# Two-layer graph attention: layer 1's scores from fp16 parts, its pipeline deepened by one row, one subtraction moved to GpSimd

## The reference

```python
h = jnp.maximum(_layernorm(x, axis=-1), 0.0)
q, k, v = split_heads(h @ Wq), split_heads(h @ Wk), split_heads(h @ Wv)
sim = jnp.einsum('bhid,bhjd->bhij', q, k) * scale
sim = jnp.where(adjacency_mask[:, None, :, :], sim, neg)
attn = jax.nn.softmax(sim, axis=-1)
out = jnp.einsum('bhij,bhjd->bhid', attn, v)     # heads side by side again
x = x + out @ Wo + bo
```

## Time and profile before

| | |
|---|---|
| median of 3 runs | 2652.82 us (2652.71 to 2655.8) |
| the profiled execution | 2656.29 us, span 2654.5 us |
| PE busy | 2587.7 us, 97% of the span |
| DVE busy | 1990.9 us, 75% |
| ACT busy | 1754.5 us, 66% |
| POOL busy | 1399.6 us, 53% |
| share of 16 DMA engines | 69.0% |

### The profile page before, as it was taken

One profiled execution on the slowest core, in us unless ns is written; L12 is line 12 of the kernel. 1 busy time (PEld: TensorE's weight loads), 2 busy tenths in 40 slices (PEclk: granted clock), 3 DMA queues, 4 the chain that ended last, 5 costly groups with the idle time before them and its releaser, 6 DMA issues. The chain is left out here.

```text
span 2654.5 us, 62516 instructions
## 1 busy us (share of the span) xinstructions
PE 2587.7 (97%) x20882; PEld 1393.6 (52%) x20886; DVE 1990.9 (75%) x6361; ACT 1754.5 (66%) x5020; POOL 1399.6 (53%) x2790
## 2 busy tenths in 40 slices
PE   6999999999999999999999999997999999999998
PEld 3455555555555555555555555554555555555554
DVE  6477778777877777777777777786777777777766
ACT  3566666666666666666666666675777777777774
POOL 4255545545554555555555555544565656555552
PEclk9999999999999999999999999998999999999999
DMA  5367766776667666766776677678786777778774
GB/s 141 61 136 158 144 135 133 149 155 130 145 141 140 145 128 144 149 142 133 141 147 141 131 140 146 148 141 195 158 175 160 169 163 170 164 160 170 158 149 102
DMA packets 945489, 387.43 MB, mean 146 GB/s; under 512 B 857617, under 2 KB 859153, under 8 KB 945169
## 3 DMA queue, kind: packets, MB, share of 16 engines
q1 hardware_dynamic: 945168, 383.44, 69.0%
HBM read 114.86 MB, written 67.11 MB: 69 GB/s over the span
## 5 line engine op out<-in xcount | busy, mean ns | idle before, releaser
L552 ACT ACTIVATE probs<-probs,negmax 128x128 f32<-128x128 f32 x1024 | 398.2, 390 | 455.6 <-DVE negmax L124 455.6
L465 POOL TENSOR_TENSOR o_sb<-o_sb,xres 128x512 f32<-128x512 f32 x127 | 161.5, 1272 | 496.5 <-DVE o_sb L739 493.1
L166 PE MATMUL l_ps_pj<-hT,room 128*128 128x512 f16 x1488 | 346.7, 383 | 2.3 <-ACT room L1343 2.3
L166 PE MATMUL ps_pj<-wm_hi,hT 128*128 128x512 f16 x1024 | 326.4, 380 | 12.6 <-DVE wm_lo L761 6.8
L166 PE MATMUL ps_pj<-wv_hi,hT 128*128 128x512 f16 x1024 | 326.4, 380 | 0.0
L166 PE MATMUL ps_pj<-hT,wk_hi 128*128 128x512 f16 x1024 | 305.9, 380 | 0.0
L166 PE MATMUL ps_pj<-hT,wq_hi 128*128 128x512 f16 x1024 | 304.5, 379 | 0.0
L1357 ACT ACTIVATE l_probs<-l_probs,l_negmax 128x128 f32<-128x128 f32 x512 | 199.2, 390 | 139.0 <-DVE l_negmax L124 138.8
L1292 POOL TENSOR_TENSOR l_h<-l_h 128x512 f16<-128x512 f32 x120 | 139.6, 1164 | 282.3 <-DVE l_out_sb L1440 245.0
L124 DVE CUSTOM_DVE_ANT_0 probs<-ps_sc,mask 128x128 f32<-128x128 f32 x1024 | 235.4, 285 | 47.4 <-PE ps_sc L981 46.7
L721 DVE SCALAR_TENSOR_TENSOR c<-cprobs,c 128x512 f16<-128x512 f32 x256 | 185.2, 723 | 79.6 <-ACT c L559 79.2
(11 more groups left out here) (172 smaller groups left out, 6198.8 us busy)
## 6 DMA issues: line engine op xcount, KB each, us to landing
xg<-in_x SPq DMA_DIRECT2D x128, 256.0 KB, 3.4
xres<-in_x SPq DMA_DIRECT2D x128, 256.0 KB, 3.1
x_scratch<-o_sb SPq DMA_DIRECT2D x128, 256.0 KB, 2.4
out<-l_out_sb SPq DMA_DIRECT2D x128, 256.0 KB, 3.3
l_ring<-x_scratch SPq DMA_DIRECT2D x124, 256.0 KB, 3.2
mask_u<-in_adj SPq DMA_DIRECT2D x64, 64.0 KB, 2.8
cpT<-c SPq DMA_TRANSPOSE x256, 3.2
xg<-x_scratch SPq DMA_DIRECT2D x12, 256.0 KB, 3.2
```

What stands on the lines that cost most here:

```text
L166: last = pe.matmul(out, a(kt), b(kt), start=(n == 0), stop=(n == 3 * kts - 1))
L465: nc.gpsimd.tensor_tensor(o_sb[:, j % 2], o_sb[:, j % 2], xres[:, j % 2], ALU.add).then_inc(res_done, 1)
L552: last = nc.scalar.activation(probs[:, i], probs[:, i], ACT.Exp, bias=negmax[:, u % 2, i:i + 1], scale=-1.0, accum_out=zsum[:, u % 4, hh:h ...
```

## The change

The scores of layer 1 are made of three fp16 products per pair of heads in place of one f32 product. For that the projections of q and k are no longer scaled and copied in f32: ScalarE writes their high part (`qk_high`), VectorE the low part (`qk_low`), and the scale is applied in `mask_scores`. The mask's value for excluded pairs is scaled to match. Projections run five rows ahead (`LEAD`), h one row further ahead, `weigh_values` three rows behind (`LAG`). The probabilities have four places instead of one (`nprobs`) and two (`p16`), v has three groups of places, the ring of rows 22 places. The factor 2^14 on the probabilities is applied through the reciprocal, for which `normalise` has one more small multiply. `p_low` is an instruction of GpSimd, first in its pass. The `factors` stand in the passes with n % 4 == 0.

```diff
 # numbers of places and passes
-RING = 20
+RING = 22
+LEAD = 5
+LAG = 3
 # mask_scores: the scale is an argument
-... mask, -1.0, FLOAT_MAX, ALU.add, ALU.min, negmax[:, i:i + 1])
+... mask, scale, FLOAT_MAX, ALU.add, ALU.min, negmax[:, i:i + 1])
 # layer 0, last group
+            def qk1_low(c):
+                dve.wait_ge(qkhi1_done, c + 1)
+                kind = "qk"[c % 2]
+                nc.vector.tensor_tensor(next_layer["qk_lo"][kind][:, 0, c // 2], ps_pj[0][:], next_layer["qk_hi"][kind][:, 0, c // 2],
+                                        ALU.subtract).then_inc(qklo1_done, 1)
...
                     if u >= QUAD:
                         v1_low(u - QUAD)
+                    else:
+                        qk1_low(u)
 # layer 1, SyncE
-                first = n + 9 < B and (n + 9) % QUAD
+                first = n + 10 < B and (n + 10) % QUAD
 # layer 1, GpSimd
+            def p_low(n):
+                pool.wait_ge(phi_done, count(n + 1))
+                nc.gpsimd.tensor_tensor(p16[:, n % 4, 1], nprobs[:, n % 4], p16[:, n % 4, 0], ALU.subtract).then_inc(plo_done, 1)
...
             for n in range(B):
-                if n + 9 < B:
-                    h_low(n + 9)
+                p_low(n)
+                if n + 10 < B:
+                    h_low(n + 10)
                 if n >= 3:
                     add_bias(n - 3)
-                if n % QUAD == 1 and n + 11 < B:
-                    factors(n + 11)
+                if n % QUAD == 0 and n + 12 < B:
+                    factors(n + 12)
 # layer 1, ScalarE
-            def qk_copy(i):
+            def qk_high(i):
...
+                nc.scalar.copy(qk_hi["qk"[c % 2]][:, g % 2, c // 2], ps_pj[0][:]).then_inc(qkhi_done, 1)
...
-                nc.scalar.activation(p16[:, n % 2, 0], nprobs[:], ACT.Copy, scale=F16_SCALE).then_inc(phi_done, 1)
+                nc.scalar.activation(p16[:, n % 4, 0], nprobs[:, n % 4], ACT.Copy).then_inc(phi_done, 1)
...
+            for n in range(B - LEAD):
+                qk_high(n + LEAD)
+                if n + 11 < B:
+                    relu(n + 11)
+                    h_high(n + 11)
                 exps(n + 1)
+                v_high(n + LEAD)
+                if n >= LAG:
+                    aT_high(n - LAG)
                 p_high(n + 1)
 # layer 1, VectorE
+            def qk_low(i):
+                g, c = divmod(i, QUAD)
+                kind = "qk"[c % 2]
+                dve.wait_ge(qkhi_done, count(i + 1))
+                nc.vector.tensor_tensor(qk_lo[kind][:, g % 2, c // 2], ps_pj[0][:], qk_hi[kind][:, g % 2, c // 2],
+                                        ALU.subtract).then_inc(qklo_done, 1)
...
-                nc.vector.reciprocal(rec[:], zsum[:, n % 2]).then_inc(rec_done, 1)
+                nc.vector.tensor_scalar(rec[:], zsum[:, n % 2], 1.0 / F16_SCALE, None, ALU.mult).then_inc(rec_done, 1)
+                dve.wait_ge(rec_done, count(2 * n + 1))
+                nc.vector.reciprocal(rec[:], rec[:]).then_inc(rec_done, 1)
...
+            for n in range(B - LEAD):
+                qk_low(n + LEAD)
+                if n >= LEAD:
+                    add_residual(n - LEAD)
                 row_max(n + 1)
+                if n + 16 < B:
+                    stats(n + 16)
                 normalise(n + 1)
+                v_low(n + LEAD)
+                if n >= LAG:
+                    aT_low(n - LAG)
 # layer 1, TensorE
                 for pr in range(PAIRS1):
-                    for b in range(2):
-                        rows = slice(DH * b, DH * b + DH)
-                        mm = nc.tensor.matmul(ps_s[:, b, pr * P:(pr + 1) * P], q_sb[rows, g % 2, pr, cols], k_sb[rows, g % 2, pr, cols],
-                                              start=True, stop=True)
+                    for i, (q_part, k_part) in enumerate(((qk_hi, qk_hi), (qk_hi, qk_lo), (qk_lo, qk_hi))):
+                        for b in range(2):
+                            rows = slice(DH * b, DH * b + DH)
+                            mm = nc.tensor.matmul(ps_s[:, b, pr * P:(pr + 1) * P], q_part["q"][rows, g % 2, pr, cols],
+                                                  k_part["k"][rows, g % 2, pr, cols], start=(i == 0), stop=(i == 2))
...
             scores(0)
+            project_qk(QUAD)
+            project_v(QUAD)
+            for n in range(B - LEAD):
+                project_qk(n + LEAD)
+                if n >= LEAD:
+                    project_out(n - LEAD)
+                scores(n + 1)
+                project_v(n + LEAD)
+                if n >= LAG:
+                    weigh_values(n - LAG)
```

More of the change, by code:

```diff
@@ L1248, in _ @@
             transpose_h(MADE)
-            load_x(HELD + 3)
+            transpose_h(MADE + 1)
+            load_x(HELD + 4)
             sp.dma_start(bo_rows[:], bo.partition_broadcast(P)).then_inc(bo_loaded, 16)
-            load_x(HELD + 4)
+            load_x(HELD + 5)
             for n in range(B):
                 t = n // QUAD
-                first = n + 9 < B and (n + 9) % QUAD
+                first = n + 10 < B and (n + 10) % QUAD
                 if first:
-                    transpose_h(n + 9)
+                    transpose_h(n + 10)
                 transpose_p(n)
[L1258 to L1261, removed]
+                if n + 10 < B and not first:
+                    transpose_h(n + 10)
+                if n + 18 < B:
+                    load_x(n + 18)
                 for i in range(2 * n, min(2 * n + 2, MADE)):
@@ L1372, in _ @@
             exps(0)
+            qk_high(QUAD)
+            v_high(QUAD)
             p_high(0)
[L1374 to L1382, removed]
+            for i in range(MADE, MADE + 3):
+                relu(i)
+                h_high(i)
+            for n in range(B - LEAD):
[3 more added lines that the diff above has]
+                    h_high(n + 11)
                 exps(n + 1)
-                v_high(n + QUAD)
-                if n >= 2:
-                    aT_high(n - 2)
+                v_high(n + LEAD)
+                if n >= LAG:
+                    aT_high(n - LAG)
                 p_high(n + 1)
-            for n in range(B - QUAD, B - 1):
+            for n in range(B - LEAD, B - 1):
                 exps(n + 1)
                 p_high(n + 1)
-                aT_high(n - 2)
-            for i in range(B - 3, B):
+                aT_high(n - LAG)
+            for i in range(B - 1 - LAG, B):
                 aT_high(i)
@@ L1443, in _ @@
             row_max(0)
+            qk_low(QUAD)
             normalise(0)
-            p_low(0)
-            for i in range(HELD, 15):
+            v_low(QUAD)
+            for i in range(HELD, HELD + QUAD):
                 stats(i)
-            for n in range(B - QUAD):
-                if n >= 4:
-                    add_residual(n - 4)
+            for n in range(B - LEAD):
+                qk_low(n + LEAD)
+                if n >= LEAD:
+                    add_residual(n - LEAD)
                 row_max(n + 1)
-                if n + 15 < B:
-                    stats(n + 15)
+                if n + 16 < B:
+                    stats(n + 16)
                 normalise(n + 1)
-                v_low(n + QUAD)
-                if n >= 2:
-                    aT_low(n - 2)
-                p_low(n + 1)
-            row_max(B - 3)
-            for n in range(B - QUAD, B - 1):
-                add_residual(n - 4)
+                v_low(n + LEAD)
+                if n >= LAG:
+                    aT_low(n - LAG)
+            row_max(B - LEAD + 1)
+            for n in range(B - LEAD, B - 1):
+                add_residual(n - LEAD)
                 normalise(n + 1)
@@ L1464, in _ @@
                     row_max(n + 2)
-                p_low(n + 1)
-                aT_low(n - 2)
-            for i in range(B - 5, B - 2):
+                aT_low(n - LAG)
+            for i in range(B - LEAD - 1, B - 2):
                 add_residual(i)
@@ L1567, in build @@
         keys = 2 * KT * D
-        v_hi, v_lo = (sb(f"l1_v_{part}", [P, 2, QUAD, INNER], F16) for part in ("hi", "lo"))
+        v_hi, v_lo = (sb(f"l1_v_{part}", [P, 3, QUAD, INNER], F16) for part in ("hi", "lo"))
+        qk_parts = [room[:, start:start + 2 * PAIRS1 * D].bitcast(F16).rearrange("p (s g b n) -> p s g b n", s=2, g=2, b=PAIRS1)
+                    for start in (0, keys)]
         parts = room[:, 2 * keys:].bitcast(F16).rearrange("p (n c) -> p n c", n=8)
```

141 lines of the change are left out of this document (63 added, 78 removed).

## The result

| | before | after |
|---|---|---|
| median | 2654.06 us (2652.71 to 2655.8, 4 runs) | 2687.49 us (2686.93 to 2688.52, 4 runs) |
| span of the profiled execution | 2654.5 us | 2685.9 us |
| PE busy | 2587.7 us, 97% | 2568.6 us, 96% |
| DVE busy | 1990.9 us, 75% | 2024.0 us, 75% |
| ACT busy | 1754.5 us, 66% | 1736.4 us, 65% |

The ratio is 1.0126, 95% interval 1.0108 to 1.0144. The direction was forecast; the size was not: +33.4 us where +13 were forecast, and the time lies over the range's upper end of 2681.

What follows compares the result with a forecast made beforehand. TensorE's list of matmuls, 6.51 us a row in layer 1, was taken as the bound. The profiled 2656.3 + 11.9 (late GpSimd steps) + 1.5 (layer 0) = 2669.7, and 3.5 over the median gave 2666 us, range 2650 to 2681.

Steps and rivals of the forecast that it cites:

- TensorE's scores, 0.65 to 0.43: Layer 1's scores on TensorE: fp16 takes 0.43 us for 0.65, saving 0.22 per row, so TensorE alone needs 6.29.
- The ring: ScalarE and VectorE, qk_high through row_max and exps to p_high and back: 6.17 us a row, hidden below TensorE's 6.29.
- row_max to exps 0.97: Layer 1, from the start of VectorE's row_max to the start of exps: 0.97 us, taken from the trace before.
- The late factors: GpSimd's layer-norm steps queue behind p_high: relu waits 2.3 us, a later multiply is held, 1.76 us lost per four rows.
- The multiply on zsum: VectorE's added 128x4 multiply in normalise: 0.19 us with hand-over, but stopped until add_bias ends in one row of four.
- the multiply is not stopped: Rival: the added VectorE multiply runs through GpSimd's add_bias, a group takes 26.04 us, the kernel 2654 us; chance 0.17.
- TensorE stays the bound: Rival: layer-norm steps end in time or idle time is taken up; rows cost 6.29 us, the kernel 2628; chance 0.09.
- Further stops, 2676 to 2695: Rival: more GpSimd and VectorE meetings, a late transpose holding h_high, or add_residual at 0.79: 2676 to 2695 us; chance 0.18.
- Layer 0, forecast as untouched: Layer 0 ahead of its last four half rows: the prediction's sum has no term for it.
- Start and end of layer 1: One row moves from the end to the time ahead of the pass: about 4 us each way, 0 within 4.
- The four qk1_low: Layer 0's last four half rows get one each: at most 4 x 0.60, partly covered by ScalarE's list, +1.5 us.
- The signs of being wrong: Profile after: relu waits for nothing, rows even at 6.3, or TensorE's waits end on another engine's work than VectorE's.

Runs made afterwards that it cites:

- the version that fills TensorE: The changed kernel with qk_high ahead of p_high on ScalarE and the 17 layer-norm steps cut into 9 and 8 over two GpSimd passes: 2637.24 us, ratio 0.9928.
- scale_const: The changed kernel with the scale in layer 1's row_max as the constant -1.0, scores left unscaled: 2675.83 us, ratio 1.0068.
- split_scale_const: The changed kernel with the 17 layer-norm steps cut into 9 and 8 and row_max's scale as the constant -1.0, scores left unscaled: 2638.0 us, ratio 0.9933.
- factors_split: The changed kernel with the 17 layer-norm steps cut in two, 9 in the GpSimd pass before and 8 where all were: 2654.42 us, ratio 0.9994.
- factors_early: The changed kernel with all 17 layer-norm steps one GpSimd pass earlier: 2681.89 us, ratio 1.0096.
- plow_last: The changed kernel with p_low last in GpSimd's pass instead of first: 2699.08 us, ratio 1.0158.
- plow_on_vector: The changed kernel with p_low back on VectorE, behind aT_low's place in the pass: 2703.65 us, ratio 1.0174.

## Why the prediction was right in kind and wrong in size

Against the span of before, the profile after is 31.4 us longer, where the prediction's terms sum to 13.4. By the starts of layer 0's casts of probabilities and of layer 1's p_high, the 18 us between them are:

| part | forecast | measured |
|---|---|---|
| layer 0 up to its last group | 0 | +6.7 |
| last group of layer 0 | +1.5 | +2.6 |
| from there to row 9 of layer 1 | 0 within 4 | +4.8 |
| rows 9 to 122, 113 rows | +11.3 (0.10 each) | +21.0 (6.695 against 6.509) |
| from row 122 to the end | 0 within 4, and the last 0.6 of the +11.9 | -3.7 |

The medians are another 3.3 us further from the forecast: the profiled execution of before lay 3.5 over its median, which the prediction took off, and that of the change lay 0.25 over its own.

- **TensorE's scores, 0.65 to 0.43:** right, 0.45 in the version that fills TensorE, and 6.30 a row for 6.29.
- **The ring, 6.17 us:** the same nine steps in the same order, eight of them within 0.02 of the forecast. This is the step that failed: "row_max to exps 0.97". The prediction carried the duration of the earlier trace rows over to an instruction whose constant the diff turns into a per-partition operand, and named no bound for it. It measured 1.19. scale_const shows that the operand is the cause, and split_scale_const that 6.18 would have hidden. With the operand out, the time is 2675.83, inside the range; so this term is what took the time over 2681. It is not the whole miss: that kernel has the forecast group of 26.4 and is still 18.7 us over the kernel before on its chip, where 13 were forecast. In its profile, as in that of the change, most of the rest lies in layer 0 (5.9 us).
- **The late factors, 1.76 per group:** right in place, order and both parts (the relu's wait, the multiply held by add_bias), wrong in size: 1.09. The relu waited 1.77 for 2.3, mostly because the ring is 0.26 longer: the relu is wanted later, and the gap ahead of exps (1.13 in a plain row) is wider too. Without the operand the row loses about 1.6. The rest is the 17 steps, which took 4.90 from first to last start (2212.78 to 2217.68) where 5.1 was taken. The two errors partly cancel: 26.44 was forecast, 26.82 came, and 26.41 without the operand.
- **The multiply on zsum:** held until add_bias ends, as forecast (0.61 for 0.15 to 0.17), in 28 rows; the rival "the multiply is not stopped" is out. The page "SBUF — State Buffer" of the Trainium skill, in Who interferes with whom, says that a VectorE instruction with two SBUF inputs contends with a GpSimd instruction that reads SBUF. The trace agrees: the product takes 1.50 for 0.69 in two of the runs, while qk_low at 2209.74, with one input in PSUM, is 0.69 inside p_low's 2209.31 + 1.16. The multiply has only one tensor as input, so its hold is not a case of this sentence; it rests on the runs.
- **"TensorE stays the bound":** out for the change. Its condition was stated rightly: factors_split brings the group to 25.72, and only with the ring under 6.3 as well do rows cost 6.30.
- **"Further stops, 2676 to 2695":** the time lies in its range, but by luck. No product was held, and add_residual starts row_max after 0.66, as in the sum. h_high waited for a transpose in 7 rows, at most 0.68, which is less than the gap of 1.13 ahead of exps.
- **Layer 0, forecast as untouched:** the prediction put it at nothing without a reason, and it is 6.7 of the 18 us. All ten profiles of changed kernels reach its end later than the first of before, by 0.6 to 7.3 us. From half row 128 to 208, where no instruction was changed, they take 533.0 to 538.9 us; the two of before take 532.3 and 533.2, so two of the ten lie with them, and part of the lag can be spread. The medians say the same: those of the ten lie 4.6 to 15.0 us over what rows 9 to 122 account for. The cause stays open; no run here isolates it (the memory layout does differ).
- **Start and end of layer 1:** the row that moves to the start costs 4.8 and the end gives 3.7 back, the "about 4 us each way" of the prediction. The four qk1_low cost at most 2.6 with what surrounds them (2.1 to 2.7 in the ten profiles), 1.5 forecast.
- **The signs of being wrong:** none came true. The relu waits, the rows are not even (6.43 and 7.52 for about 6.2 and 7.9), and TensorE's waits end on VectorE's v_low. The mechanism was right; sizes were off, one in the ring and one in layer 0.

## What to carry to other kernels

When an edit makes one engine's list shorter, sum the ring of the others instruction by instruction, and price anew each instruction whose operands the diff changes, not only those that it adds: here 0.06 us on each of four instructions, 0.25 a row, decided between 16 us gained and none. Work that comes every fourth row has a due time: late, it costs a wait, and early but in one piece it makes its engine late for the next rows and collides there. Cutting it in two pieces of nine and eight steps in two passes took away both. A cast that waits for its input (p_high) stands better behind one that is ready (qk_high), if the ready one is in the ring.

## What the runs showed of the hardware

- VectorE's masked row maximum (128x128, PSUM and SBUF in) takes 0.28 or 0.29 and starts 0.20 to 0.22 after the one before when its scale is a constant (the kernel before, scale_const), and 0.34 or 0.35 and 0.26 to 0.28 when the scale is read per partition from SBUF (the change).
- A multiply of 128x4 is not small when GpSimd subtracts or adds 128x512 in SBUF: 0.34, 0.61, 0.86 and 1.11 in place of 0.17 (factors_early, the change, plow_last, plow_on_vector), each ending within 0.03 of the GpSimd instruction. The product behind it then met the next GpSimd instruction in two of these kernels (1.50 in place of 0.69 in factors_early and plow_last).
